# Causal mask as a GpSimd select after the exp, score steps in pairs, and one ring of six PSUM banks in a fused attention kernel

## The chip, the cores and the metric

One Trainium2 chip, one of its cores. The metric is the device time of one launch in microseconds, as the median of several runs; lower is better.

## The reference

The input x has 8 batches of 1024 tokens and 512 channels; it is normalised over the channels. On that, causal attention with 16 heads of 64 is computed, with two learned null keys and values for each head, and a layer norm of the normalised input is added (the second branch, of which only the norm term is computed here).

```python
q = (layernorm(x) @ Wq);  kv = x @ Wkv
k, v = concat(null_k, k), concat(null_v, v)
sim = 8 * l2norm(q) * q_scale @ (l2norm(k) * k_scale).T
sim = sim - slope[h] * abs(j - i)
sim = where(j > i, -inf, sim)
out = x + softmax(sim) @ v @ Wout + yn
```

## The kernel before

All of the work is in `fused_block`, written out by hand for each engine, with semaphores between them. Matmuls run on float16 in high and low parts: of each product three terms are taken (high by high, low by high, high by low).

A **unit** is one batch and one pair of heads, so there are 64 units (`NU`). A unit passes through these stages:

- Projection (`proj`, L1236 to L1238): 8 token tiles, each 12 matmuls of 388 columns into one PSUM bank. ScalarE (L566, L569) and VectorE (L1046, L1047) empty it.
- Norms of q and k: ScalarE squares (L584), VectorE sums (L1119, L1122), GpSimd takes the power and multiplies (L803, L809, L815, L820: the norm block), ScalarE and VectorE write the high and low float16 part (L574, L1054), a transposing DMA turns them into `KQ`.
- Pieces: a plain product of q and k (L1283), 12 pieces of 128 to 512 keys for each head, only to find each row's maximum. VectorE adds the distance term and takes the maximum (L1034), one operation per head and piece.
- Scores, ten steps m = 0 to 9 (`STEPS`), keys on the partitions and up to 512 queries in the free dimension: six matmuls with q and k (L1259) and two that add the distance term and minus the maximum (L1263), for each block of 128 keys. Heads 0 and 1 stand in rows 0 to 63 and 64 to 127 of TensorE and write to two neighbouring banks. Steps 2 and 9 hold two blocks each. Six steps (0, 1, 2, 7, 8, 9) hold the diagonal, eight blocks in all.
- The mask: for each of these blocks four matmuls of 64 columns (L1294) add -1e30 above the diagonal, with the tables `TRI` and `IDB`. They are issued after the pieces of the same slot.
- ScalarE takes the exp from PSUM into `PR`, float32 (L598), and directly behind it casts it to float16 into `PH` (L602). The low part `PL` is the difference: steps 0, 4 and 7 on GpSimd (L792), the others on VectorE (L1075). `PR` has two buffers, so the exp of step m+2 waits for the low part of step m.
- Values: three matmuls of 66, 64 and 66 columns for each block, head and query tile (L1322, L1324, L1326) into two banks `AV`. Null keys come first (L1305).
- Output projection, for each pair of units: 8 tiles of 6 matmuls of 512 columns (L1349 to L1351), added to `ACC` by VectorE (L1112).

The order of each engine's program is set by tables of slot numbers. A unit has 48 slots (`SL`); `due(s, W_...)` yields the items whose slot is s, so that stages of about four units are interleaved. Engines are not tied to each other by the slots, only by semaphores, and each runs its program strictly in order.

PSUM has eight banks. Two (`SB`) belong to the score steps: a step waits until the exp of the step before is done (`s_p`). Two belong to `AV`. Four are a ring for pieces, projections and output tiles: `ring_order` assigns the banks ahead of time, and `bank_free` waits for whoever reads the bank's last content.

## Time and profile before

| what | value |
|---|---|
| median of 3 runs | 2699.8 us (2696.74 to 2699.81) |
| profiled execution, span from first to last instruction | 2696.2 us |
| TensorE busy | 2622.8 us, 97% |
| VectorE busy | 2488.1 us, 92% |
| ScalarE busy | 2126.7 us, 79% |
| GpSimd busy | 2098.1 us, 78% |

The page gives the span of the profiled execution and no time of its own around it; the runs beside it lie 0.5 to 3.6 us above that span. Busy time is the union of an engine's instructions. Matmuls overlap, so a matmul's duration in a row is its way through the array, and how long it holds up the next one is seen from the starts.

### The profile page before, as it was taken

Reading aid. Unit: us, or ns where it says so; the run is one execution under the profiler, and the core shown is the slowest. Engines: PE = TensorE matmul, PEld = TensorE weight load, DVE = VectorE, ACT = ScalarE, POOL = GpSimd, SP = SyncE. Lnnn points to the kernel's source line nnn. Section 1 sums busy time; section 2 is a strip of 40 time slices with the busy share of each in tenths; the row PEclk is TensorE's granted clock in tenths of the full one; section 3 lists DMA queues with packets and bytes.
Section 4 is the critical chain, followed back from the end, with each engine's and each line's share of the span. In section 5 each row is a group of like instructions: output and inputs, shape, how many; then the busy total and the mean of one; then the engine's idle time right before and its main releaser. Section 6 shows DMA issues by size and latency. Waiting matters only on the chain.

```text
span 2696.2 us, 84329 instructions
## 1 busy us (share of the span) xinstructions
PE 2622.8 (97%) x31631; PEld 1575.9 (58%) x31631; DVE 2488.1 (92%) x6760; ACT 2126.7 (79%) x3385; POOL 2098.1 (78%) x2438
## 2 busy tenths in 40 slices
PE   5799999999999999999999999999999999999997
PEld 4455565565565565565555565565655665565654
...
GB/s 177 67 63 74 81 102 99 91 71 82 102 100 94 69 87 98 96 87 76 90 107 82 93 75 101 100 95 71 80 107 87 100 74 76 98 100 80 54 59 71
DMA packets 638790, 236.94 MB, mean 88 GB/s; under 512 B 594609, under 2 KB 596657, under 8 KB 638385
## 3 DMA queue, kind: packets, MB, share of 16 engines
q1 hardware_dynamic: 636912, 231.45, 39.6%
...
q10 hardware_dynamic: 1472, 0.09, 0.0%
...
## 4 chain that ended last, share of the span: by engine, by line
PE 81%; DVE 7%; issue 3%; DMA 2%; POOL 1%; SPq 1%; ACT 1%; DVEq 0%; POOLq 0%; ACTq 0%
PE PS L1259 12%; PE PS L1236 11%; PE PS L1238 10%; PE PS L1237 10%; PE PS L1283 6%; PE PS L1322 6%; PE PS L1326 4%; PE PS L1324 4%; PE PS L1263 4%; PE PS L1349 4%; PE PS L1350 3%; PE PS L1351 3%; DVE PS L1034 3%; DVE AR L1075 1%; PE PS L1294 1%
## 5 line engine op out<-in xcount | busy, mean ns | idle before, releaser
L1034 DVE CUSTOM_DVE_ANT_0 PS<-PS,STR 128x512 f32<-128x512 f32 (+3 forms) x1536 | 822.5, 580 | 121.9 <-PE PS L1283 114.9
L598 ACT ACTIVATE AR<-PS,SC 128x1024 f32<-128x1024 f32 (+1 forms) x640 | 655.1, 1024 | 143.5 <-PE PS L1294 75.7
L1236 PE MATMUL PS<-WH,XT 128*128 128x388 f16 x2048 | 676.7, 330 | 22.5 <-DVE AR L1047 13.5
L1237 PE MATMUL PS<-WL,XT 128*128 128x388 f16 x2048 | 673.9, 329 | 0.0
L1238 PE MATMUL PS<-WH,XT 128*128 128x388 f16 x2048 | 673.7, 329 | 0.0
L602 ACT ACTIVATE AR<-AR 128x1024 f16<-128x1024 f32 (+1 forms) x640 | 622.0, 972 | 20.3
L803 POOL TENSOR_TENSOR RN<-SS,HALF 128x8 f32<-128x8 f32 x256 | 453.6, 1772 | 182.7 <-DVE SS L1122 181.6
L1075 DVE TENSOR_TENSOR AR<-AR 128x768 f16<-128x768 f32 (+1 forms) x448 | 503.4, 1134 | 11.8 <-ACT AR L602 11.7
L1259 PE MATMUL PS<-AR 64*128 64x512 f16 (+3 forms) x4608 | 495.4, 324 | 9.1 <-ACT AR L598 8.9
L1322 PE MATMUL PS<-AR 128*128 128x66 f16 x4608 | 472.3, 195 | 1.8 <-DVE AR L1075 0.8
L1324 PE MATMUL PS<-AR 128*128 128x64 f16 x4608 | 468.8, 192 | 0.0
L1326 PE MATMUL PS<-AR 128*128 128x66 f16 x4608 | 466.3, 193 | 0.0
L1322 PEld LDWEIGHTS PS<-AR 128*128 128x128 f16 x4608 | 414.8, 97 | 71.5 <-issue 41.3
L792 POOL TENSOR_TENSOR AR<-AR 128x1024 f16<-128x1024 f32 x192 | 412.8, 2150 | 20.2 <-ACT AR L602 19.6
L1324 PEld LDWEIGHTS PS<-AR 128*128 128x128 f16 x4608 | 420.0, 99 | 8.6
L1326 PEld LDWEIGHTS PS<-AR 128*128 128x128 f16 x4608 | 420.3, 97 | 0.0
L566 ACT ACTIVATE QKB<-PS 128x128 f32<-128x128 f32 x512 | 139.7, 273 | 266.0 <-PE PS L1238 260.3
L1236 PEld LDWEIGHTS PS<-WH,XT 128*128 128x128 f16 x2048 | 200.5, 98 | 198.4 <-issue 55.6
L815 POOL TENSOR_TENSOR SQ<-QKB,RN 128x512 f32<-128x512 f32 x256 | 292.1, 1141 | 0.0
L796 POOL TENSOR_TENSOR OTK<-OTOK,OTK 128x512 f16<-128x512 f32 x128 | 163.1, 1275 | 152.5 <-ACT OTK L591 150.9
L1238 PEld LDWEIGHTS PS<-WH,XT 128*128 128x128 f16 x2048 | 201.0, 98 | 138.2 <-issue 2.9
L1259 PEld LDWEIGHTS PS<-AR 64*128 64x128 f16 x4608 | 199.6, 94 | 135.1 <-ACT AR L598 25.6
...
## 6 DMA issues: line engine op xcount, KB each, us to landing
XW<-in_L_attn_x SPq DMA_DIRECT2D x112, 256.0 KB, 3.0
...
AR<-QKB SPq DMA_TRANSPOSE x512, 2.5
...
```

The costliest lines, as they stand in the source:

```text
L598: e.activation(PR[:, n % 2, :, 0:wide], SB[:, :, 0:wide], ACT.Exp, scale=SIG).then_inc(s_p, 1)
L602: e.activation(PH[:, n % 3, :, 0:wide], PR[:, n % 2, :, 0:wide], ACT.Copy).then_inc(s_ph, 1)
L803: e.tensor_tensor(RN[:, i % 2, :], SS[:, i % 2, :], HALF[:, :], ALU.pow).then_inc(s_rn, 1)
L1034: e.tensor_tensor_reduce(out=r[:, 0:n], in0=r[:, 0:n], in1=ST[:, u % 2, h, o:o + n], scale=1.0, scalar=LOW, op0=ALU.add, op1=ALU.max, accu ...
L1075: e.tensor_tensor(PL[:, n % 3, :, 0:wide], PR[:, n % 2, :, 0:wide], PH[:, n % 3, :, 0:wide], ALU.subtract).then_inc(s_pl, 1)
L1236: e.matmul(to, XT[:, k, xs], WH[:, k, p, :], start=k == 0, stop=False)
L1237: e.matmul(to, XT[:, k, xs], WL[:, k, p, :], start=False, stop=False)
L1238: ins = e.matmul(to, XT[:, 4 + k, xs], WH[:, k, p, :], start=False, stop=k == KC - 1)
L1259: e.matmul(SB[:, h, to], KQ[hs, u % 2, a, ks], KQ[hs, u % 2, c, qs], start=(a, c) == (KH, QH) and not off, stop=False, skip_group_check=True)
L1322: e.matmul(AV[:, h, 66 * q:66 * q + 66], PH[:, n % 3, h, pq], VV[:, 0:66], start=False, stop=False, skip_group_check=True)
L1324: e.matmul(AV[:, h, 66 * q:66 * q + 64], PH[:, n % 3, h, pq], VV[:, 72:136], start=False, stop=False, skip_group_check=True)
L1326: ins = e.matmul(AV[:, h, 66 * q:66 * q + 66], PL[:, n % 3, h, pq], VV[:, 0:66], start=False, stop=kt == 4 * qc + q, skip_group_check=True)
```

## The change

- The mask matmuls and their tables go. After the exp, GpSimd sets the entries above the diagonal to zero in `PR` (`affine_select`, L817 of the changed kernel), one instruction for each of the six diagonal steps, over both heads and all blocks of the step. The cast of that step waits for it.
- The product that adds the distance term gets one more term for far entries (`FAR`, in `CTK` and `AL`); its matmuls stay the same in number and size.
- The exp and the cast of a step have separate slot tables (`W_SCORE`, `W_CAST`).
- `SB` goes. Pieces, projections, output tiles and score steps share a ring of six banks; `take_pair` gives a score step two neighbouring ones, and `bank_free` waits for their last readers.
- The 12 pieces are put in 10 groups; small ones share a pair of banks. The maxima of a group wait for its last matmul.
- All slot tables are new, and a unit has 50 slots.

```diff
-BANKS = 4
-SL = 48
+BANKS = 6
+SL = 50
...
-NEG = -1e30
 LOW = -3e38
+FAR = 32768.0
...
-PIECES = [(qt, c) for qt in range(NT) for c in range(1 + qt // 4)]
+GROUPS = [[(0, 0), (2, 0)], [(3, 0)], [(1, 0)], [(4, 0)], [(5, 0)], [(4, 1), (6, 1)], [(6, 0)], [(5, 1)], [(7, 0)], [(7, 1)]]
...
+DIAGONAL = [blocks[0][0] >= 4 * qc for qc, blocks in STEPS]
...
-W_PIECE = [47, 53, 56, 59, 66, 68, 69, 77, 79, 82, 83, 86]
-W_SCORE = [88, 96, 105, 108, 111, 115, 118, 126, 130, 133]
+W_PIECE = [54, 54, 61, 67, 68, 80, 80, 84, 92, 92]
+W_SCORE = [98, 98, 109, 109, 112, 112, 124, 124, 136, 136]
+W_CAST = [100, 101, 110, 111, 116, 116, 126, 127, 138, 142]
+W_CAUS = [101, 103, 109, 128, 136, 138]
...
-HOLD = [2.0, 2.1, 2.0, 6.7]
...
+HOLD = [11.9, 12.5, 14.5, 14.3, 14.8]
...
+def pieces(g):
+
+    out, at = [], 0
+    done = 2 * sum(len(z) for z in GROUPS[:g])
+    for qt, c in GROUPS[g]:
+        n = min(512, P * (qt + 1) - 512 * c)
+        out.append((qt, c, at, n, done))
+        at += n
+        done += 2
+    return out
 
...
+    def take_pair(slot, u, m):
+        i = min(range(BANKS - 1), key=lambda z: (max(read[z], read[z + 1]), read[z] + read[z + 1]))
+        for h in range(2):
+            who = ("sc", u, 2 * m + h)
+            at[who], before[who] = i + h, last[i + h]
+            last[i + h], read[i + h] = who, slot
+
...
-        SB, AV = PS[:, 0:2, :], PS[:, 2:4, 0:264]
+        AV = PS[:, 6:8, 0:264]
...
-                e.wait_ge(s_mx, 24 * u + i + 1)
+                e.wait_ge(s_mx, 24 * u + pieces(i // 2)[-1][4] + i % 2 + 1)
+            elif what == "sc":
+                e.wait_ge(s_p, NS * u + i // 2 + 1)
...
+                    low = BANK["sc", u, 2 * m]
                     w.wait_ge(s_st, 2 * n + 2)
                     w.wait_ge(s_wo, 8)
                     pl_done(w, n - 2)
-                    e.activation(PR[:, n % 2, :, 0:wide], SB[:, :, 0:wide], ACT.Exp, scale=SIG).then_inc(s_p, 1)
+                    e.activation(PR[:, n % 2, :, 0:wide], PS[:, low:low + 2, 0:wide], ACT.Exp, scale=SIG).then_inc(s_p, 1)
+                for u, m in due(s, W_CAST):
+                    n = NS * u + m
+                    wide = width(m)
                     w.wait_ge(s_p, n + 1)
+                    cut = causal(n)
+                    if DIAGONAL[m]:
+                        w.wait_ge(s_caus, cut + 1)
                     if n > 2:
                         w.wait_ge(s_av, n - 2)
...
+            for r in range(4):
+                pc(e.memset(CTK[0:64, :, r, 35 + 4 * r::64], FAR))
...
-            pc(e.memset(IDB[:, :], 0.0))
-            pc(e.affine_select(out=IDB[:, :], in_=IDB[:, :], compare_op=ALU.not_equal, fill=1.0, base=0,
-                               pattern=[[-1, P]], channel_multiplier=1))
-            pc(e.memset(TRI[:, :, :], 0.0))
-            for a in range(2):
-                pc(e.affine_select(out=TRI[:, a, :], in_=TRI[:, a, :], compare_op=ALU.is_ge, fill=NEG, base=64 * a - 64,
-                                   pattern=[[-1, P]], channel_multiplier=1))
-            pc(e.memset(TRI[0:64, :, :], 0.0))
-            pc(e.affine_select(out=TRI[0:64, 0, :], in_=TRI[0:64, 0, :], compare_op=ALU.is_ge, fill=NEG, base=0,
-                               pattern=[[-1, P]], channel_multiplier=1))
-            e.affine_select(out=TRI[0:64, 1, :], in_=TRI[0:64, 1, :], compare_op=ALU.is_ge, fill=NEG, base=64,
-                            pattern=[[-1, P]], channel_multiplier=1).then_inc(s_tri, 1)
             w.wait_ge(s_ready, 1)
...
+                for u, i in due(s, W_CAUS):
+                    m = [z for z in range(NS) if DIAGONAL[z]][i]
+                    n = NS * u + m
+                    two = len(STEPS[m][1])
+                    own = PR[:, n % 2, :, 0:256 * two].rearrange("p h (t c) -> p h t c", c=256)[:, :, :, 0:P]
+                    w.wait_ge(s_p, n + 1)
+                    e.affine_select(out=own, in_=own, compare_op=ALU.is_ge, fill=0.0, base=0,
+                                    pattern=[[0, 2], [0, two], [1, P]], channel_multiplier=-1).then_inc(s_caus, 1)
                 for u, m in due(s, W_PLOW):
...
+                        for h in range(2):
+                            far = ALF.rearrange("p (j k) -> p j k", k=P)[:, 4:8, 64:P]
+                            e.affine_select(out=far, in_=far, compare_op=ALU.not_equal, fill=-FAR, base=-(64 * h + 35),
+                                            pattern=[[-4, 4], [0, 64]], channel_multiplier=1).then_inc(s_ald, 1)
+                            w.wait_ge(s_ald, 2 + h)
...
-                    w.wait_ge(s_s, 24 * u + 2 * i + 2)
-                    w.wait_ge(s_str, 2 * u + 2)
-                    if u:
-                        w.wait_ge(s_m, 3 * (2 * (u - 1) + qt // 4) + 3)
-                    for h in range(2):
-                        r = rb("s", u, 2 * i + h)
-                        e.tensor_tensor_reduce(out=r[:, 0:n], in0=r[:, 0:n], in1=ST[:, u % 2, h, o:o + n], scale=1.0, scalar=LOW,
-                                               op0=ALU.add, op1=ALU.max,
-                                               accum_out=MX[:, qt // 4, qt % 4, h, c:c + 1]).then_inc(s_mx, 1)
+                    for qt, c, at, n, done in pieces(i):
+                        o = 896 - P * qt + 512 * c
+                        w.wait_ge(s_s, 24 * u + pieces(i)[-1][4] + 2)
+                        w.wait_ge(s_str, 2 * u + 2)
+                        if u:
+                            w.wait_ge(s_m, 3 * (2 * (u - 1) + qt // 4) + 3)
+                        for h in range(2):
+                            r = rb("s", u, 2 * i + h)
+                            e.tensor_tensor_reduce(out=r[:, at:at + n], in0=r[:, at:at + n], in1=ST[:, u % 2, h, o:o + n], scale=1.0,
+                                                   scalar=LOW, op0=ALU.add, op1=ALU.max,
...
+                for u, i in due(s, W_PIECE):
+                    bank_free(w, "s", u, 2 * i)
+                    bank_free(w, "s", u, 2 * i + 1)
+                    for qt, c, at, n, done in pieces(i):
+                        for g in range(qt // 2 + 1):
+                            w.wait_ge(s_kq[g], 32 * (u + 1))
+                        for h in range(2):
+                            hs = slice(64 * h, 64 * h + 64)
+                            e.matmul(rb("s", u, 2 * i + h)[:, at:at + n], KQ[hs, u % 2, QH, P * qt:P * qt + P],
+                                     KQ[hs, u % 2, KH, 512 * c:512 * c + n], start=not at, stop=True,
+                                     skip_group_check=True).then_inc(s_s, 1)
...
                     qc, blocks = STEPS[m]
-                    n = NS * u + m
-                    w.wait_ge(s_p, n)
+                    low = BANK["sc", u, 2 * m]
+                    bank_free(w, "sc", u, 2 * m)
+                    bank_free(w, "sc", u, 2 * m + 1)
                     for g in range(max(2 * qc + 1, blocks[-1][0] // 2) + 1):
...
-                                e.matmul(SB[:, h, to], KQ[hs, u % 2, a, ks], KQ[hs, u % 2, c, qs],
+                                e.matmul(PS[:, low + h, to], KQ[hs, u % 2, a, ks], KQ[hs, u % 2, c, qs],
                                          start=(a, c) == (KH, QH) and not off, stop=False, skip_group_check=True)
...
-                            ins = e.matmul(SB[:, h, to], AL[hs, kt - 4 * qc + 4, :], CT[hs, u % 2, qs], start=False,
-                                           stop=kt < 4 * qc, skip_group_check=True)
-                            if kt < 4 * qc:
+                            ins = e.matmul(PS[:, low + h, to], AL[hs, kt - 4 * qc + 4, :], CT[hs, u % 2, qs], start=False,
+                                           stop=True, skip_group_check=True)
+                            if kt == blocks[-1][0]:
                                 ins.then_inc(s_st, 1)
...
-                    if blocks[0][0] >= 4 * qc:
-                        w.wait_ge(s_tri, 1)
-                        for kt, off in blocks:
-                            for a in range(2):
-                                for h in range(2):
-                                    hs = slice(64 * h, 64 * h + 64)
-                                    to = slice(off + 64 * a, off + 64 * a + 64)
-                                    ins = e.matmul(SB[:, h, to], TRI[hs, a, :], IDB[hs, hs], start=False, stop=True,
-                                                   skip_group_check=True)
-                                    if a and kt == blocks[-1][0]:
-                                        ins.then_inc(s_st, 1)
...
-                    if blocks[0][0] == 0:
-                        w.wait_ge(s_nv2, 2 * u + qc + 1)
```

The orders below are of the middle of the program. First TensorE, around step 2 of a unit (two diagonal blocks). Before: L1236 to L1238 are projections, L1283 a piece, L1259 and L1263 scores, L1294 the mask, L1305 null keys.

```order
L1238 MATMUL PS<-WH,XT 128x388
L1283 MATMUL PS<-AR 128x384 x2
L1259 MATMUL PS<-AR 128x256 x6
L1263 MATMUL PS<-AR,AL 128x256 x2
L1259 MATMUL PS<-AR 128x128 x6
L1263 MATMUL PS<-AR,AL 128x128 x2
L1294 MATMUL PS<-IDB,TRI 128x64 x8
L1305 MATMUL PS<-VNT,PNT 128x264 x2
L1236 MATMUL PS<-WH,XT 128x388
```

Now, with L1274 as a projection, L1375 an output tile, L1316 and L1320 as scores, L1331 null keys, L1296 pieces, L1346 values:

```order
L1375 MATMUL PS<-WO,OT 128x512
L1316 MATMUL PS<-AR 128x256 x6
L1320 MATMUL PS<-AR,AL 128x256 x2
L1316 MATMUL PS<-AR 128x128 x6
L1320 MATMUL PS<-AR,AL 128x128 x2
L1316 MATMUL PS<-AR 128x512 x6
L1320 MATMUL PS<-AR,AL 128x512 x2
L1331 MATMUL PS<-VNT,PNT 128x264 x2
L1296 MATMUL PS<-AR 128x256 x2
L1346 MATMUL PS<-AR 128x66
```

The mask rows are gone, two steps follow each other with nothing between them, and the pieces stand by themselves.

ScalarE, with what each waits for. Before, L598 is the exp and L602 the cast (L566 and L569 empty a projection tile, L584 squares):

```order
L566 ACTIVATE QKB<-PS 128x128 [waits s_proj]
L569 ACTIVATE AR<-PS,VSC 128x2x64
L598 ACTIVATE AR<-PS,SC 128x2x384 [waits s_pl,s_st]
L602 ACTIVATE AR<-AR 128x2x384 [waits s_av,s_p]
L574 ACTIVATE QKB<-SQ 128x2x256 [waits s_t1]
L584 ACTIVATE SQ<-QKB 128x512 [waits s_hi,s_ss,s_lo,s_qb,s_kvev]
```

Now, L628 is the exp, L638 the cast, L595 and L598 empty a projection tile, L613 squares, L620 casts the output:

```order
L595 ACTIVATE QKB<-PS 128x128 [waits s_proj]
L598 ACTIVATE AR<-PS,VSC 128x2x64
L628 ACTIVATE AR<-PS,SC 128x2x384 [waits s_plp,s_st]
L628 ACTIVATE AR<-PS,SC 128x1024 [waits s_pl,s_st]
L638 ACTIVATE AR<-AR 128x2x384 [waits s_av,s_caus,s_p]
L638 ACTIVATE AR<-AR 128x1024 [waits s_av,s_p]
L613 ACTIVATE SQ<-QKB 128x512 [waits s_hi,s_ss,s_lo,s_qb,s_kvev]
```

Two exps come ahead of two casts, and the cast of a diagonal step waits for `s_caus`, the select.

GpSimd, with what each waits for: L817 is the select, L837 to L854 the norm block, L826 the low part of step 7.

```order
L817 AFFINE_SELECT AR<-AR 128x2x128 [waits s_p]
L837 TENSOR_TENSOR RN<-SS,HALF 128x8 [waits s_nsc,s_ss]
L843 TENSOR_TENSOR NSC<-QKB,RN 128x8 [waits s_rn]
L849 TENSOR_TENSOR SQ<-QKB,RN 128x512
L854 TENSOR_TENSOR SQ<-SQ,W2R 128x2x128 [waits s_t1]
L826 TENSOR_TENSOR AR<-AR 128x1024 [waits s_av,s_ph]
L817 AFFINE_SELECT AR<-AR 128x2x128 [waits s_p]
L817 AFFINE_SELECT AR<-AR 128x4x128 [waits s_p]
L837 TENSOR_TENSOR RN<-SS,HALF 128x8 [waits s_nsc,s_ss]
```

Before, the same engine has the norm block and the low part, and no select:

```order
L803 TENSOR_TENSOR RN<-SS,HALF 128x8 [waits s_nsc,s_ss]
L809 TENSOR_TENSOR NSC<-QKB,RN 128x8 [waits s_rn]
L815 TENSOR_TENSOR SQ<-QKB,RN 128x512
L820 TENSOR_TENSOR SQ<-SQ,W2R 128x2x128 [waits s_t1]
L731 TENSOR_TENSOR XHL<-XW,XHL 128x512 [waits s_xh]
L792 TENSOR_TENSOR AR<-AR 128x1024 [waits s_av,s_ph]
```

Three selects of a unit stand around a norm block and a low part that ran without them.

## Rows read from the trace of the kernel before

**Rows 1.** The page: busy time by engine, and the chain that ended last.

```profile
PE 2622.8 (97%) x31631; PEld 1575.9 (58%) x31631; DVE 2488.1 (92%) x6760; ACT 2126.7 (79%) x3385; POOL 2098.1 (78%) x2438
...
PE 81%; DVE 7%; issue 3%; DMA 2%; POOL 1%; SPq 1%; ACT 1%; DVEq 0%; POOLq 0%; ACTq 0%
```

**Rows 2.** Busy time in three stretches: PE, PEld, DVE, ACT, POOL, clock, DMA share, GB/s.

```profile
60.00:110.00 50.00, 29.20 (x141) 14.31 (x141) 45.56 (x109) 26.91 (x55) 25.98 (x31) 0.80 0.33 83
500.00:1000.00 500.00, 498.87 (x6111) 300.20 (x6109) 468.68 (x1287) 402.20 (x643) 401.86 (x465) 1.00 0.41 87
2640.00:2697.00 57.00, 42.75 (x647) 25.92 (x646) 33.78 (x71) 33.64 (x38) 25.47 (x22) 1.00 0.27 73
```

**Rows 3.** One line, the mask matmuls: duration min/median/max in ns, first and last start.

```profile
L1294 PE MATMUL PS<-IDB,TRI x2048: 187/190/190, 114.8 to 2680.1; 64*128 64x64 bf16 x187
```

**Rows 4.** Groups by line, TensorE: busy us, mean ns, then idle before and who ended it.

```profile
L1236 PE MATMUL PS<-WH,XT 128*128 128x388 f16 x2048 | 676.7, 330 | 22.5 <-DVE AR L1047 13.5 <-DVE MX L1018 6.7 <-DVE MX L1034 2.2
...
L1259 PE MATMUL PS<-AR 64*128 64x512 f16 (+3 forms) x4608 | 495.4, 324 | 9.1 <-ACT AR L598 8.9
...
L1283 PE MATMUL PS<-AR 64*128 64x512 f16 (+3 forms) x1536 | 258.2, 330 | 16.3 <-DVE MX L1034 12.5 <-DMA AR<-QKB 1.4 <-DVE ACC L1112 1.1
```

**Rows 5.** Timeline, TensorE, around 1009 us: start, duration, line.

```profile
1008.79 0.28 PE L1294 MATMUL PS<-IDB,TRI 64*128 64x64 bf16 x8
1008.90 0.28 PE L1305 MATMUL PS<-VNT,PNT 64*128 64x264 f16 x2
```

**Rows 6.** Timeline, TensorE, around 1011 us.

```profile
1010.77 0.33 PE L1237 MATMUL PS<-WL,XT 128*128 128x388 f16 x1
1010.93 0.33 PE L1238 MATMUL PS<-WH,XT 128*128 128x388 f16 x1
1011.19 0.39 PE L1283 MATMUL PS<-AR 64*128 64x512 f16 x2
1011.42 0.81 PE L1259 MATMUL PS<-AR 64*128 64x512 f16 x6
1012.06 0.38 PE L1263 MATMUL PS<-AR,AL 64*128 64x512 f16 x2
1012.38 0.20 PE L1322 MATMUL PS<-AR 128*128 128x66 f16 x1
```

**Rows 7.** Timeline, GpSimd: three selects of the program's start.

```profile
5.98 0.29 POOL L658 TENSOR_SCALAR_AFFINE_SELECT IDF<-IDF 128x128 f32<-128x128 f32 x1 [0.17 <-POOL IDF L657]
...
32.71 1.04 POOL L753 TENSOR_SCALAR_AFFINE_SELECT DS<-DS 128x1024 bf16<-128x1024 bf16 x1 [0.15 <-POOL DS L752]
...
52.21 0.67 POOL L771 TENSOR_SCALAR_AFFINE_SELECT IDB<-IDB 128x128 bf16<-128x128 bf16 x1
```

**Rows 8.** Groups by line, ScalarE and VectorE: exp, cast, low part.

```profile
L598 ACT ACTIVATE AR<-PS,SC 128x1024 f32<-128x1024 f32 (+1 forms) x640 | 655.1, 1024 | 143.5 <-PE PS L1294 75.7 <-PE PS L1263 57.7 <-POOL AR L792 5.2
L602 ACT ACTIVATE AR<-AR 128x1024 f16<-128x1024 f32 (+1 forms) x640 | 622.0, 972 | 20.3
...
L1075 DVE TENSOR_TENSOR AR<-AR 128x768 f16<-128x768 f32 (+1 forms) x448 | 503.4, 1134 | 11.8 <-ACT AR L602 11.7
```

**Rows 9.** Groups by line, GpSimd.

```profile
L803 POOL TENSOR_TENSOR RN<-SS,HALF 128x8 f32<-128x8 f32 x256 | 453.6, 1772 | 182.7 <-DVE SS L1122 181.6
L792 POOL TENSOR_TENSOR AR<-AR 128x1024 f16<-128x1024 f32 x192 | 412.8, 2150 | 20.2 <-ACT AR L602 19.6
L815 POOL TENSOR_TENSOR SQ<-QKB,RN 128x512 f32<-128x512 f32 x256 | 292.1, 1141 | 0.0
```

**Rows 10.** Groups by line, VectorE: two operations on SBUF.

```profile
L1054 DVE TENSOR_TENSOR QKB<-SQ,QKB 128x512 f16<-128x512 f32 x256 | 211.5, 826 | 2.9 <-ACT QKB L574 2.3
...
L1122 DVE SCALAR_TENSOR_TENSOR SS<-SS,CL 128x8 f32<-128x8 f32 x256 | 92.2, 360 | 8.8
```

**Rows 11.** Two lines of VectorE: duration min/median/max in ns.

```profile
L1122 DVE SCALAR_TENSOR_TENSOR SS<-SS,CL x256: 166/169/1285, 72.6 to 2632.0; 128x8 f32<-128x8 f32 x128
...
L1034 DVE CUSTOM_DVE_ANT_0 PS<-PS,STR x1536: 277/637/735, 85.2 to 2655.6; 128x512 f32<-128x512 f32 x128, 128x128 f32<-128x128 f32 x64
```

156 lines of the change are left out of this document (72 added, 84 removed).

## The prediction

> **What bounds the kernel now.** I read the page's busy shares first: TensorE 97%, VectorE 92%, ScalarE 79%, GpSimd 78% [rows 1]. A matmul's end is modelled and matmuls overlap, so 97% does not by itself say that TensorE is the limit. The table of stretches does: from 500 to 1000 us TensorE has 498.87 of 500 us, VectorE 468.68, ScalarE 402.20, GpSimd 401.86, all at the full granted clock (1.00, the 2.4 GHz level) [rows 2]. Only the two ends are different: in 60 to 110 us TensorE has 29.20 of 50, with the clock at 0.80 and VectorE at 45.56; in the last 57 us it has 42.75. So for some 2500 us TensorE's own work sets the pace, about 40 us for each of the 64 units (the mask matmuls of all units lie between 114.8 and 2680.1 us [rows 3]).
>
> The chain of waits agrees, 81% of it is TensorE [rows 1]. The groups by line tell how little it waits for others: 9.1 us before the score matmuls, nearly all for ScalarE's exp, 16.3 us before the pieces, nearly all for VectorE's max, 22.5 us before the projections, mostly for VectorE too [rows 4]. So the question for every edit is what it takes from or adds to TensorE's row, and whether it makes a wait that is not there now.
>
> **What the change takes from TensorE.** The mask matmuls, L1294: 2048 of 64 columns. Their row says 190 ns each [rows 3], but that is the time through the array, not the time they hold it up. That is read from starts: eight of them begin at 1008.79 and the next matmul begins at 1008.90 [rows 5], 0.11 us for eight, 14 ns each (rounding of the starts: 13 to 15). 2048 x 13.75 ns = 28 us. The eight stand between other matmuls on 64 rows, so no change of shape goes with them.
> A page would give more: the Trainium skill, TensorEngine Tiling (Array Packing), section Instruction Overhead, says that a matmul with one column takes as long as one with 60, about 60 cycles. At 2.4 GHz that is an estimate of 25 ns for each, 51 us for 2048, and the forecast would be 23 us lower. The row's 0.11 us for eight speaks against counting each alone, because the two heads' matmuls stand in different row halves and run together.
>
> The second cost is shape switches. Projection matmuls follow each other after 0.16 us (starts at 1010.77, 1010.93), yet L1283, on 64 rows, starts 0.26 us after the last of them, at 1011.19 [rows 6]. So a change from 128 rows to 64 costs 0.10 us. On the way back, a pair of 512 columns gives way to another on 64 rows after 0.23 us (1011.19, 1011.42), but to L1322 on 128 rows after 0.32 (1012.06, 1012.38): 0.09 again. Gathering score steps in pairs and pieces in groups ought to save such switches. Counted in the two orders, it hardly does: about 1284 before and 1276 now, 20 a unit in both, because pieces no longer ride along with a score step. 8 x 0.10 = 1 us.
>
> **Score steps in six banks.** Today a score step waits for the exp of the step before (one pair of banks). That has cost 9 us in all [rows 4]. The pair now comes from the ring, and two steps may stand in PSUM at once; ScalarE's order puts two exps ahead of two casts. But the same six banks also serve pieces, projections and output tiles, 4 of 6 can be held by two waiting score steps, and the bank may be one that VectorE has yet to read. Bounds: all 9.1 + 16.3 us of waits go, or as much comes back. I take 5 us off.
>
> **What GpSimd gets.** Six selects a unit, 384 in all: four over 2 x 128 elements and two over 4 x 128 per partition. The trace has no float32 select of that size. Nearest: 128 elements float32 0.29 us, 1024 bfloat16 1.04 us, so 0.84 ns an element and 0.40 and 0.61 us for ours; and 128 bfloat16 0.67 us, at a time when the tables of the program's start were being made [rows 7], 0.38 more, so 0.78 and 0.99 us. A unit gets 4 x 0.40 + 2 x 0.61 = 2.8 us, or at the high end 5.1 us; 64 units, 180 to 330 us. GpSimd's 2098 us become 2280 to 2430, 85 to 91% of the span. It is not the bound by its sum, so I count this at nothing. Its cover is ScalarE's slack of some 7 us a unit (402 of 500 us busy). A unit's steps are 4 us apart in the mean, and a diagonal step now takes exp, select, cast, low part: 1.0 + 0.5 + 1.0, and 1.1 on VectorE or 2.15 on GpSimd [rows 8, 9]; two float32 buffers allow 8 us between an exp and the end of its low part. What is late next if the cover goes is the cast, and behind it on ScalarE the evacuations that free the ring. The new waits on that queue are two: the cast for the select, and the pair of exps for the low part two steps back.
>
> **What VectorE gets.** The same 24 maxima, now read group by group; its sum does not move. But it shares something with GpSimd. L1122, 8 elements, has a median of 169 ns, yet a mean of 360 and a maximum of 1285; the max on PSUM (L1034) has 637 and at most 735 [rows 10, 11]. L1075, L1054 and L1122, 503 + 212 + 92 of 2696 us, 30%, are such operations on SBUF. If a select meets one in 30% of cases, VectorE loses 0.3 x 2.8 to 5.1 = 0.8 to 1.5 us a unit, on 37.5 (0.937 of 40). That stays below TensorE's 39.6, but a little will reach it through bank waits: 5 us in all.
>
> **Ends.** Building the two mask tables on GpSimd (L771 on, from 52.21 us) goes, and four short memsets and two selects on the position table come; VectorE is the busy one there [rows 2, 7], so 0. In the tail, exp, score and exp wait for each other in turn; pairs shorten that by a score step or two of about 1 us (1011.42 to 1012.38 [rows 6]), the selects lengthen it by 0.5 each: 0.
>
> **Sum** against the profiled span: 2696.2 - 28 - 1 - 5 + 5 = 2667.2 us. The page gives no time of its own around the span; the three runs have a median of 2699.8, 3.6 above it. So **2671 us**. A measurement of this kernel tells about 0.2% from no change, 5.4 us: 2694.4 to 2705.2 is "same".
>
> **Rivals.**
> 1. The rest of TensorE's waits goes as well, since a burst of score steps needs nothing and the ring has six banks: another 11 to 20 us beyond the forecast, down to 2650. For it: 25 us of waits named above. Against: the 16.3 us are VectorE's, which gets no faster.
> 2. The gain is eaten. TensorE's order is now lumpier (two score steps, then up to 48 value matmuls, then pieces that take four banks), and each group's maxima wait for its last matmul. A new wait of 0.2 to 0.45 us a unit gives back 13 to 28 us: 2682 to 2705.
> 3. VectorE becomes the bound by being shut out. If every select holds VectorE up for its whole length, VectorE has 37.5 + 2.8 = 40.3 us a unit against 40 now: 0.3 x 64 = 19 us slower, 2719. The max and the reads of PSUM, over half of its time, show no such effect, which speaks against "every".
> The Trainium skill, SBUF — State Buffer, section SBUF: two separate sides, states the rule: a VectorE operation with two SBUF inputs and a GpSimd operation that reads SBUF exclude each other for the whole instruction. By that rule, the trace agrees in L1122, whose 169 ns become up to 1285.
> 4. The select comes late: slower. GpSimd runs in order, and its norm block holds L803 and L815, 1.77 + 1.14 = 2.9 us, and two shorter ones [rows 9]; in the new order it stands right ahead of a unit's selects and of the low part of step 7, which the exp of step 9 waits for. If a select is late, the cast waits, and the evacuations behind it, and TensorE's next bank. It decides from 29/64 = 0.45 us a unit on TensorE. At one L815 a unit, 1.14 us, it costs 73 us: 2671 + 73 = 2744. Against it: GpSimd now waits 181.6 us for VectorE's sums before L803 [rows 9], so it is usually early.
> That the mask stays on TensorE is excluded: the new order has no such matmul.
>
> **How the numbers follow.** Forecast, 2660 to 2682: 0.42. Rival 1, below 2660: 0.13. Rival 2: 0.22, of which 0.12 still ends below 2694.4 and 0.10 within 0.2%. Rival 3: 0.08. Rival 4: 0.15. Faster 0.67, same 0.10, slower 0.23. The range 2652 to 2716 leaves out some 0.05 below and 0.15 above (most of rival 4 and the end of rival 3); by costs alone it is 2650 (all waits gone) to 2719.
>
> **What would show it.** Right: no bf16 matmul rows; TensorE's busy time down by 25 to 30 us; the stretch 500 to 1000 still at 497 or more; selects at 0.4 to 0.8 and 0.6 to 1.0 us, GpSimd at 85 to 91%; VectorE's busy time up by under 60 us, in L1122's and L1054's counterparts. Wrong: TensorE below 99% in the middle, with idle time before score or piece matmuls put down to exp or max; ScalarE's casts waiting for the select by more than 60 us in all; VectorE at 97% or more.

## Result, and the profile after

2925.0 us (median of 4 runs, 2918.8 to 2928.0) against 2699.6 before: ratio 1.0831, 95% interval 1.0814 to 1.0847. The change makes the kernel slower by 225 us; 2671 was forecast. The profiled execution has a span of 2922.6 us, 226.4 above the one before.

The page of the changed kernel, busy time by engine:

```profile
PE 2630.9 (90%) x29583; PEld 1510.3 (52%) x29583; DVE 2762.8 (95%) x6760; ACT 2089.0 (71%) x3385; POOL 2470.4 (85%) x2820
```

The stretches that answer to [rows 2] (same columns; the last is the program's end):

```profile
60.00:110.00 50.00, 20.62 (x97) 10.27 (x97) 33.94 (x71) 23.49 (x46) 20.26 (x22) 0.66 0.29 74
500.00:1000.00 500.00, 461.04 (x5245) 264.10 (x5240) 480.50 (x1186) 362.72 (x587) 432.02 (x487) 1.00 0.39 83
2850.00:2923.00 73.00, 54.84 (x690) 30.19 (x690) 46.16 (x83) 37.22 (x44) 38.72 (x38) 0.90 0.26 64
```

The mask's matmuls are gone (29583 in place of 31631), but TensorE's time isn't: in the middle it is busy for 461.04 of 500 us where it had 498.87, and the clock there is 1.00 in both. VectorE now has 480.50, up from 468.68, although it finishes fewer units in that time. So the bound has moved. By the starts of each unit's first projection matmul (L1236 before, L1274 after), unit 5 begins 22.8 us later than before, the 58 units from there to unit 63 take 2541.7 us in place of 2352.0 (43.8 each in place of 40.6), and from the start of unit 63 to the end it is 121.2 us in place of 107.4: 22.8 + 189.8 + 13.8 = 226.4.

The groups of the changed kernel by line, which answer to [rows 4, 8, 9, 10] (L1316 are the first score matmuls, L1296 the pieces, L628 exp, L638 cast, L1113 VectorE's low part, L826 GpSimd's, L817 the selects, L1092 and L1160 the counterparts of L1054 and L1122):

```profile
L628 ACT ACTIVATE AR<-PS,SC 128x1024 f32<-128x1024 f32 (+1 forms) x640 | 644.9, 1026 | 407.8 <-DVE AR L1113 198.5 <-PE PS L1320 116.8 <-POOL AR L826 89.8
L1113 DVE TENSOR_TENSOR AR<-AR 128x768 f16<-128x768 f32 (+1 forms) x448 | 638.1, 1435 | 9.4 <-ACT AR L638 9.4
L638 ACT ACTIVATE AR<-AR 128x1024 f16<-128x1024 f32 (+1 forms) x640 | 597.0, 967 | 35.2 <-POOL AR L817 18.3 <-PE PS L1350 11.1 <-issue 4.5
L1316 PE MATMUL PS<-AR 64*128 64x512 f16 (+3 forms) x4608 | 495.0, 325 | 37.3 <-DVE MX L1072 21.0 <-issue 12.6 <-DMA AR<-CTK 1.7
...
L837 POOL TENSOR_TENSOR RN<-SS,HALF 128x8 f32<-128x8 f32 x256 | 425.6, 1662 | 65.5 <-DVE SS L1160 61.4
L826 POOL TENSOR_TENSOR AR<-AR 128x1024 f16<-128x1024 f32 x192 | 424.8, 2213 | 16.7 <-ACT AR L638 14.6
...
L849 POOL TENSOR_TENSOR SQ<-QKB,RN 128x512 f32<-128x512 f32 x256 | 344.0, 1344 | 0.0
L1092 DVE TENSOR_TENSOR QKB<-SQ,QKB 128x512 f16<-128x512 f32 x256 | 279.5, 1092 | 14.6 <-ACT QKB L603 14.6
...
L817 POOL TENSOR_SCALAR_AFFINE_SELECT AR<-AR 128x256 f32<-128x256 f32 (+1 forms) x384 | 220.5, 574 | 233.2 <-ACT AR L628 229.2
...
L1296 PE MATMUL PS<-AR 64*128 64x512 f16 (+3 forms) x1536 | 210.6, 330 | 153.5 <-DVE ACC L1150 48.7 <-DVE AR L1085 42.6 <-ACT AR L628 35.6
...
L1160 DVE SCALAR_TENSOR_TENSOR SS<-SS,CL 128x8 f32<-128x8 f32 x256 | 105.7, 413 | 8.8
```

VectorE's low part takes 1435 ns in the mean where it took 1134, L1092 1092 where it took 826, and VectorE's busy sum rises from 2488.1 to 2762.8 us. Who waits is to be read in the idle columns: exp is idle for 407.8 us (143.5 before), 198.5 of them until VectorE's low part two steps back is done, 89.8 until GpSimd's; the pieces wait 153.5 us (16.3), and GpSimd's own idle time before L837 has shrunk from 182.7 to 65.5.

How an operation of VectorE becomes long shows in the timeline of VectorE, GpSimd and ScalarE at 905 us (start, duration, in brackets the wait ahead of it and who ended it):

```profile
905.55 2.13 POOL L826 TENSOR_TENSOR AR<-AR 128x1024 f16<-128x1024 f32 x1
...
905.71 3.05 DVE L1113 TENSOR_TENSOR AR<-AR 128x1024 f16<-128x1024 f32 x1
...
908.86 1.69 ACT L628 ACTIVATE AR<-PS,SC 128x768 f32<-128x768 f32 x2 [1.14 <-DVE AR L1113]
```

GpSimd starts its low part at 905.55 and has it until 907.68; VectorE starts the low part of the other step of the pair at 905.71 and ends 3.05 us later, at 908.76. The exp that needs its buffer has waited 1.14 us by then. By my count in the records of the trace, 59 of GpSimd's 192 low parts have a low part of VectorE beside them now, and 5 of 192 had one before. All 33 of VectorE's that are longer than 2.3 us are among these. The new order did that, and mostly for one pair: in 49 of the 59 GpSimd's step 7 stands beside VectorE's step 6, in 8 step 0 beside step 1, in 2 step 4 beside step 5.

These 59 do not carry the whole rise. By the same records a low part of VectorE with nothing of GpSimd's beside it takes 1.22 us (1024 elements) or 0.95 (768); what all 448 take above that sums to 164 us (29 before), and 63 of it lie in the 59. GpSimd's low parts also stand beside L1092 now, 62 times where it was 16, and L1092 takes 1918 ns in the mean there against 828 elsewhere. Others of GpSimd's operations lengthen VectorE's low part as well: beside L830 alone (the low part of the output) 1024 elements take 2.17 to 2.18 us, 12 times.

### The profile page after: what moved, and what is told of

Read it like the earlier page. It is cut to its first block and busy times, and to the rows that moved or that the text cites. A ratio compares the mean times of both kernels' runs of the same rounds, so it can differ in the third digit from the quotient of the medians.

```text
span 2922.6 us, 80374 instructions
## 1 busy us (share of the span) xinstructions
PE 2630.9 (90%) x29583; PEld 1510.3 (52%) x29583; DVE 2762.8 (95%) x6760; ACT 2089.0 (71%) x3385; POOL 2470.4 (85%) x2820
## 5 line engine op out<-in xcount | busy, mean ns | idle before, releaser
L628 ACT ACTIVATE AR<-PS,SC 128x1024 f32<-128x1024 f32 (+1 forms) x640 | 644.9, 1026 | 407.8 <-DVE AR L1113 198.5
L1072 DVE CUSTOM_DVE_ANT_0 PS<-PS,STR 128x512 f32<-128x512 f32 (+3 forms) x1536 | 812.1, 582 | 32.0 <-PE PS L1296 30.0
L1274 PE MATMUL PS<-WH,XT 128*128 128x388 f16 x2048 | 677.7, 331 | 12.0 <-DVE MX L1057 6.7
L1113 DVE TENSOR_TENSOR AR<-AR 128x768 f16<-128x768 f32 (+1 forms) x448 | 638.1, 1435 | 9.4 <-ACT AR L638 9.4
L638 ACT ACTIVATE AR<-AR 128x1024 f16<-128x1024 f32 (+1 forms) x640 | 597.0, 967 | 35.2 <-POOL AR L817 18.3
L1316 PE MATMUL PS<-AR 64*128 64x512 f16 (+3 forms) x4608 | 495.0, 325 | 37.3 <-DVE MX L1072 21.0
L1346 PE MATMUL PS<-AR 128*128 128x66 f16 x4608 | 469.8, 195 | 29.6 <-POOL AR L826 26.0
L1346 PEld LDWEIGHTS PS<-AR 128*128 128x128 f16 x4608 | 417.9, 97 | 132.7 <-issue 102.9
L837 POOL TENSOR_TENSOR RN<-SS,HALF 128x8 f32<-128x8 f32 x256 | 425.6, 1662 | 65.5 <-DVE SS L1160 61.4
L826 POOL TENSOR_TENSOR AR<-AR 128x1024 f16<-128x1024 f32 x192 | 424.8, 2213 | 16.7 <-ACT AR L638 14.6
L817 POOL TENSOR_SCALAR_AFFINE_SELECT AR<-AR 128x256 f32<-128x256 f32 (+1 forms) x384 | 220.5, 574 | 233.2 <-ACT AR L628 229.2
L1296 PE MATMUL PS<-AR 64*128 64x512 f16 (+3 forms) x1536 | 210.6, 330 | 153.5 <-DVE ACC L1150 48.7
L849 POOL TENSOR_TENSOR SQ<-QKB,RN 128x512 f32<-128x512 f32 x256 | 344.0, 1344 | 0.0
L1316 PEld LDWEIGHTS PS<-AR 64*128 64x128 f16 x4608 | 194.6, 94 | 232.7 <-issue 66.4
L1274 PEld LDWEIGHTS PS<-WH,XT 128*128 128x128 f16 x2048 | 200.3, 98 | 202.3 <-issue 51.1
L1092 DVE TENSOR_TENSOR QKB<-SQ,QKB 128x512 f16<-128x512 f32 x256 | 279.5, 1092 | 14.6 <-ACT QKB L603 14.6
```

The source lines that it names most:

```text
L628: e.activation(PR[:, n % 2, :, 0:wide], PS[:, low:low + 2, 0:wide], ACT.Exp, scale=SIG).then_inc(s_p, 1)
L638: e.activation(PH[:, n % 3, :, 0:wide], PR[:, n % 2, :, 0:wide], ACT.Copy).then_inc(s_ph, 1)
L837: e.tensor_tensor(RN[:, i % 2, :], SS[:, i % 2, :], HALF[:, :], ALU.pow).then_inc(s_rn, 1)
L1072: e.tensor_tensor_reduce(out=r[:, at:at + n], in0=r[:, at:at + n], in1=ST[:, u % 2, h, o:o + n], scale=1.0, scalar=LOW, op0=ALU.add, op1=A ...
L1113: e.tensor_tensor(PL[:, n % 3, :, 0:wide], PR[:, n % 2, :, 0:wide], PH[:, n % 3, :, 0:wide], ALU.subtract).then_inc(s_pl, 1)
L1274: e.matmul(to, XT[:, k, xs], WH[:, k, p, :], start=k == 0, stop=False)
```

## Experiments

Three theories stood at the start. A: GpSimd's operations on SBUF, the low parts above all, hold VectorE up, and VectorE bounds the new order. H (for handshake): the select between exp and cast costs, by its wait on a queue that works in order; the expectations of e1 to e3 call it theory B. The third, their theory C: the ring of six banks makes TensorE wait in order for banks that VectorE still reads. One more came up on the way: G, that GpSimd's time costs by itself.

### The parts of the change in the old order

**e1: the kernel before, with the selects in place of TensorE's mask.** Old order and banks, with a list for the cast and one for the select, whose places I chose and did not tune:

```diff
+W_CAST = [89, 97, 106, 109, 112, 116, 119, 130, 131, 134]
+W_CAUS = [90, 93, 95, 125, 125, 126]
...
+                    if DIAGONAL[m]:
+                        w.wait_ge(s_caus, cut + 1)
```

> The kernel before with one part of the change: mask matmuls out, six GpSimd selects a unit in, the cast in a slot of its own, everything else and all other slot tables as before. Theory A (VectorE is held up because the new order puts its operations on SBUF beside GpSimd's long ones; the selects are a small part): 2665 to 2710 us, VectorE's low part stays near 1134 ns in the mean. Theory B (the select between exp and cast costs the time): 2850 or more. Theory C (the ring of six makes TensorE wait): 2665 to 2710, since the ring is not in it.

Measured: 3026.8 us, ratio 1.1218 (1.1199 to 1.1238). GpSimd, by groups:

```profile
L802 POOL TENSOR_TENSOR AR<-AR 128x1024 f16<-128x1024 f32 x192 | 409.4, 2132 | 108.4 <-ACT AR L614 107.8
...
L793 POOL TENSOR_SCALAR_AFFINE_SELECT AR<-AR 128x256 f32<-128x256 f32 (+1 forms) x384 | 240.7, 628 | 262.7 <-ACT AR L604 240.5 <-PE PS L1328 20.2
```

It waits 240.5 us for exp ahead of the selects and 107.8 for casts ahead of its low parts, where it waited 19.6 before [rows 9]. The cover of 7 us a unit on ScalarE does not carry the handshake in this order. The places may have a part in it: on GpSimd the select of step 8 stands ahead of the low part of step 7 (both in slot 125), which the exp of step 9 waits for; in the changed kernel it stands behind it. Other places were not tried.

**e2: e1 with the ring of six banks as well.**

```diff
-BANKS = 4
-HOLD = [2.0, 2.1, 2.0, 6.7]
+BANKS = 6
+HOLD = [2.0, 2.1, 2.0, 6.7, 3.0]
...
-        SB, AV = PS[:, 0:2, :], PS[:, 2:4, 0:264]
+        AV = PS[:, 6:8, 0:264]
```

> As the first run, and with the one ring of six banks for score steps too, with the old slot tables, single steps and 12 pieces. Theory A: 2660 to 2720. Theory B: 2850 or more. Theory C: 2800 or more, with TensorE waiting before pieces and scores for the banks' last readers.

Measured: 3095.5 us, ratio 1.1472 (1.1449 to 1.1495), 69 us above e1. The ring costs here too.

**e5: the kernel before, with 8 selects a unit that nobody waits for**, over 256 elements of a tile of their own; they wait for nothing but each other. The mask stays on TensorE.

```diff
+                for u, i in due(s, W_CAUS):
+                    for z in ...:
+                        e.affine_select(out=SCR[:, :], in_=SCR[:, :], ...).then_inc(s_scr, 1)
```

> The kernel before, unchanged in its result, with eight additional selects a unit of 256 elements on a scratch tile on GpSimd, which wait for nothing and for which nobody waits. Handshake theory (the select costs because exp, select and cast wait for each other in three in-order queues): 2695 to 2720 us. GpSimd-time theory (the added 3 to 5 us a unit of GpSimd work, and what it takes from VectorE, is what costs): 2800 or more.

Measured: 2811.4 us, ratio 1.0416 (1.0399 to 1.0434), 112 us slower: the 2695 to 2720 that theory H gave is missed, and G's 2800 or more holds. Operations of GpSimd that nobody waits for cost 0.41 us here for each us of theirs (273.8 us).

**e6: e5 with each of these selects waiting for its step's exp**, still with nobody waiting for them.

```diff
+                    w.wait_ge(s_p, NS * u + (0, 1, 2, 7, 8, 9)[i] + 1)
```

> The same, with each of the additional selects waiting for the exp of its diagonal step; still nobody waits for them. If it is the waiting of GpSimd for the exp that costs (what is queued behind it there comes late): 2800 to 3000. If it is the cast's wait for the select: under 2740. First run of before with selects: 3027.

Measured: 2975.5 us, ratio 1.1023 (1.1007 to 1.1039), 164 us above e5. So of the handshake the half that the prediction did not price, GpSimd standing still with other work behind it, is by itself worth more than the selects' time, in the slots of e1. What it is worth in the changed kernel's slots was not measured by itself.

**e11: e5 with powers in place of the selects**, over 2 elements each. They were meant to keep GpSimd as busy and hardly to touch SBUF.

```diff
-                        e.affine_select(out=SCR[:, :], in_=SCR[:, :], ...)
+                        e.tensor_tensor(SCR[:, 0:2], TWOS[:, 0:2], HALF[:, 0:2], ALU.pow)
```

> As e5 (the kernel before with 8 more GpSimd operations a unit that nobody waits for, +112 us), but each is a power over 2 elements, about 0.45 us by a quarter of the 1.73 us for 8 elements in e8, in place of a select over 256 elements at 0.535 us. So it adds nearly the same GpSimd time and hardly touches SBUF. Theory G (GpSimd's time is what costs: its other work comes later and TensorE waits for it): +80 to +115 us, 2780 to 2815. Theory V (the selects cost by holding VectorE up): within 20 us of before, 2690 to 2720.

Measured: 2869.5 us, ratio 1.0632 (1.0616 to 1.0648), 170 us slower. The powers took longer than I had estimated:

```profile
L602 ACT ACTIVATE AR<-PS,SC 128x1024 f32<-128x1024 f32 (+1 forms) x640 | 655.6, 1024 | 242.0 <-POOL AR L802 80.2 <-PE PS L1304 74.8 <-PE PS L1273 55.6
...
L813 POOL TENSOR_TENSOR RN<-SS,HALF 128x8 f32<-128x8 f32 x256 | 460.9, 1800 | 46.3 <-DVE SS L1132 45.5
...
L802 POOL TENSOR_TENSOR AR<-AR 128x1024 f16<-128x1024 f32 x192 | 409.7, 2134 | 18.5 <-ACT AR L606 17.9
L794 POOL TENSOR_TENSOR SCR<-TWOS,HALF 128x2 f32<-128x2 f32 x512 | 408.3, 798 | 15.1
...
L1293 PE MATMUL PS<-AR 64*128 64x512 f16 (+3 forms) x1536 | 261.5, 333 | 93.5 <-DMA AR<-QKB 41.4 <-DVE MX L1044 33.6 <-issue 10.4
```

0.80 us each, 408.3 in all, and 170 / 408 = 0.42 us for each us, e5's rate again. So V (the expectation's name for the theory that the added operations cost by their own traffic on SBUF) falls, and it is GpSimd's time that costs. VectorE is not out of it: its sum rose by 108.4 us here and by 77.5 in e5. The largest part here, 51.9 us, is in L1064 (L1054 before, 826 ns, 1029 here). Of the 126 low parts of VectorE that stood beside a power, 98 took their own time, and the other 28 all had another operation of GpSimd beside them too; so the lengthening is put down to GpSimd's own operations, which came later and stood beside others of VectorE's. TensorE's busy sum rose as well, by 31.7 us in e5 and 56.8 here, at a mean granted clock of 0.984 and 0.979 in place of 0.993; that is a part of the 112 and the 170 us. The rows say how GpSimd's time gets through although it is busy for 78% of the span: its only large reserve, 182.7 us before the norm block [rows 9], is down to 46.3; exp waits 80.2 us for its low part (5.2 before [rows 8]), and the pieces 41.4 us for the transposes of QKB, whose scaling uses GpSimd's SQ (1.4 [rows 4]).

**e10: the kernel before without GpSimd's low parts** (from the second unit on a power over 8 elements stands in for each of steps 0, 4 and 7, so these low parts are missing from the values). The edit is that of e8, below.

> The kernel before, with the same replacement as e8 alone: GpSimd's low parts of steps 0, 4 and 7 left out from the second unit on, a power over 8 elements in their place. It tells whether e8's 155 us belong to the new order or to GpSimd's low parts anywhere. Theory A (pairs put GpSimd's low part beside VectorE's): the kernel before is bound by TensorE, which loses nothing: within 0.4% of before, 2688 to 2705, VectorE's low part (L1075, here shifted by a few lines) from 1134 to about 1090 ns. Rival (GpSimd's low parts hold the kernel up in any order): over 30 us faster.

Measured: 2699.8 us, ratio 1.0000 (0.9991 to 1.0010), VectorE's low part 1146 ns. As expected: where TensorE is the bound and hardly any low parts stand side by side (5 of 192), GpSimd's can go and nothing is gained.

**e7: the kernel before with the ring alone**, e2's edit without the selects.

> The kernel before with the one ring of six banks alone: mask on TensorE, single steps, 12 pieces, old slot tables. Ring theory: 2750 or more, with TensorE waiting before scores and pieces for VectorE's maxima. Otherwise 2690 to 2720.

Measured: 2819.4 us, ratio 1.0443 (1.0427 to 1.0459), 120 us slower, with VectorE no longer than before (88%). The score matmuls:

```profile
L1272 PE MATMUL PS<-AR 64*128 64x512 f16 (+3 forms) x4608 | 497.2, 324 | 100.1 <-DVE MX L1046 57.8 <-issue 35.3 <-ACT AR L610 2.0
```

They were idle for 9.1 us, nearly all for exp [rows 4]; now it is 100.1, the largest part for VectorE's maxima, which have yet to read the bank.

**e14: e7 with other estimates of how long a bank is held.**

```diff
-HOLD = [2.0, 2.1, 2.0, 6.7, 3.0]
+HOLD = [3.0, 3.1, 3.0, 6.7, 5.0]
```

> e7 (the kernel before with one ring of six banks and nothing else) with other estimates of how long a bank is held: 3.0 slots for pieces and outputs and 5.0 for scores, in place of 2.0 and 3.0. If e7's 120 us lie in which bank is given to whom, the time moves by over 25 us, either way. If they lie in the ring itself (TensorE, in order, waits for VectorE's maxima before scores that would have had a bank of their own), it stays within 25 us of 2819, and scores wait for VectorE's maxima as before, 60 to 130 us.

Measured: 3030.2 us, ratio 1.1225 (1.1205 to 1.1244), 211 us above e7; the same matmuls wait 256.4 us, 177.3 of them for maxima. So the cost lies in which bank is given to whom, and four numbers of a table moved it by 211 us. What a ring with good estimates costs or brings in the old order stays open.

### Taking parts out of the changed kernel

**e3: the changed kernel with the mask back on TensorE**, as before the change, and no selects.

```diff
-                for u, i in due(s, W_CAUS):
-                    e.affine_select(out=own, in_=own, ...).then_inc(s_caus, 1)
...
+                                    ins = e.matmul(PS[:, low + h, to], TRI[hs, a, :], IDB[hs, hs], start=False, stop=True,
```

> The changed kernel with the mask put back on TensorE (2048 matmuls of 64 columns right behind the scores) and without the selects and the cast's wait for them; pairs, ring and slot tables as changed. Theory A: 2850 to 2950, VectorE's low part still over 1300 ns in the mean. Theory B: under 2760. Theory C: 2850 to 2950.

Measured: 2849.2 us, ratio 1.0559 (1.0538 to 1.0581), at the lower edge of A's range and far from H's: 76 us better than the change, 150 worse than before. The exchange of the mask, which is the change's first aim, loses 76 us in the new order, and two thirds of the loss are there without it. VectorE is still at 2698.6 us (95%) with a low part of 1418 ns.

**e8: the changed kernel without GpSimd's low parts** of steps 0, 4 and 7 from the second unit on; a power over 8 elements stands in their place, and they are missing from the values.

```diff
-                        e.tensor_tensor(PL[:, n % 3, :, 0:wide], PR[:, n % 2, :, 0:wide], PH[:, n % 3, :, 0:wide],
-                                        ALU.subtract).then_inc(s_plp, 1)
+                        e.tensor_tensor(DUM[:, 0:8], TWOS[:, 0:8], HALF[:, :], ALU.pow).then_inc(s_plp, 1)
```

> The changed kernel with GpSimd's low part (three a unit, 2.2 us each) replaced from the second unit on by a power over 8 elements, about 1.7 us, that hardly touches SBUF; those low parts are left out. Theory A (VectorE held up by GpSimd's long SBUF operations beside it): VectorE's low part falls from 1435 ns to 1250 or less, the counterpart of L1054 from 1092 to 900 or less, the time to 2740 to 2840. Otherwise 2880 or more.

Measured: 2769.9 us, ratio 1.0261 (1.0240 to 1.0281), 155 us better than the change. But 1.7 us stood for 2.2, so GpSimd's time had changed as well. (e4 was the same with the power in the first unit too; it has no measured time.)

**e13: e8 with a power over 11 elements**, so that GpSimd's time stays.

```diff
-                        e.tensor_tensor(DUM[:, 0:8], TWOS[:, 0:8], HALF[:, :], ALU.pow).then_inc(s_plp, 1)
+                        e.tensor_tensor(DUM[:, :], TWOS[:, :], TWOS[:, :], ALU.pow).then_inc(s_plp, 1)
```

> The changed kernel with its selects, and from the second unit on a power over 11 elements in place of each of GpSimd's low parts (those low parts are left out of the values). In e8 the power over 8 elements took 1.73 us and moved the time by 155 us, but it was also 0.5 us shorter than the low part; by the slope from 2 elements (0.80 us, e11) to 8 (1.71 us) 11 take about 2.17 us, the low part's own 2.21. So GpSimd's time stays and only its traffic on SBUF goes. Theory A (VectorE held up): nearly all of e8's gain stays, 2765 to 2810, VectorE's low part (L1113, shifted) under 1250 ns. Theory G (GpSimd's time, at about 0.41 us for each us as in e5 and e11): the gain is gone, 2880 to 2925, though VectorE's low part is short.

Measured: 2776.8 us, ratio 1.0286 (1.0271 to 1.0301). The groups:

```profile
L630 ACT ACTIVATE AR<-PS,SC 128x1024 f32<-128x1024 f32 (+1 forms) x640 | 637.8, 1026 | 259.7 <-PE PS L1327 131.6 <-POOL DUM L831 85.6 <-DVE AR L1120 38.1
...
L1120 DVE TENSOR_TENSOR AR<-AR 128x768 f16<-128x768 f32 (+1 forms) x448 | 525.2, 1181 | 12.5 <-ACT AR L640 12.5
...
L831 POOL TENSOR_TENSOR DUM<-TWOS 128x11 f32<-128x11 f32 x189 | 414.9, 2195 | 12.3 <-ACT AR L640 10.5
...
L1303 PE MATMUL PS<-AR 64*128 64x512 f16 (+3 forms) x1536 | 200.6, 329 | 60.5 <-DVE ACC L1157 17.8 <-DMA AR<-QKB 16.9 <-ACT AR L630 16.5
...
L1099 DVE TENSOR_TENSOR QKB<-SQ,QKB 128x512 f16<-128x512 f32 x256 | 183.5, 717 | 14.9 <-ACT QKB L605 14.9
```

2195 ns stand for 2213, GpSimd is as loaded (86%), and 148 of e8's 155 us stay. Two rows of the timeline, at 864 us, set against the pair at 905 us above:

```profile
863.91 2.11 POOL L831 TENSOR_TENSOR DUM<-TWOS 128x11 f32<-128x11 f32 x1
...
865.01 1.22 DVE L1120 TENSOR_TENSOR AR<-AR 128x1024 f16<-128x1024 f32 x1
```

The same low part over 1024 elements beside an equally long operation of GpSimd takes 1.22 us, not 3.05. By my count 112 of the 120 low parts beside such a power keep their own time, and the other 8 have another operation of GpSimd beside them too. VectorE's sum falls by 252.4 us to 2510.4. This is the run that decides between A and G in the new order: A. It exchanges the operation along with its size (a power over 11 elements for a subtraction over 1024), so that it is the traffic on SBUF, and not the kind of operation, is the likely reading and not shown apart.

**e12: the changed kernel with GpSimd making steps 0, 1 and 7.**

```diff
-PL_POOL = (0, 4, 7)
+PL_POOL = (0, 1, 7)
```

> The changed kernel with one number changed: GpSimd makes the low parts of steps 0, 1 and 7 in place of 0, 4 and 7, so that only one of its three stands beside the low part that VectorE makes of the other step of its pair. The result stays the kernel's. Theory A in its narrow form (the collision is with the partner's low part): VectorE's low part falls from 1435 ns to about 1320, 40 to 90 us faster, 2835 to 2885. In its wide form (GpSimd's 2.2 us hold up whatever VectorE does beside them): the hold moves to other operations, and the time stays within 40 us of 2925. Rival (the wait is what counts: GpSimd makes two low parts one after the other, and the values and the next exp wait for the second): slower, 2940 to 3000, exp waiting for GpSimd's low part over 150 us.

Measured: 2885.0 us, ratio 1.0687 (1.0669 to 1.0705), 40 us better than the change. VectorE's low part falls to 1394 ns only, and VectorE's sum by 63 us. Between the narrow form of A (40 to 90) and the wide one (within 40), it sits on the border. It does not test the pairing, though: by the same count as above 55 of GpSimd's low parts still have one of VectorE's beside them (59 in the changed kernel), all of them step 7's beside step 6's, which the edit left alone. What it took away is the company of L1092: 8 meetings with GpSimd's low part in place of 62, and 238.2 us in all in place of 279.5.

**e15: the changed kernel with all low parts on VectorE**, `PL_POOL = ()`.

> The changed kernel with one list emptied: VectorE makes all ten low parts, GpSimd none. The result stays the kernel's. GpSimd loses 425 us of work, VectorE gets 192 low parts at about 1.2 us, 230 us, and loses the hold of about 150 to 230 us. Theory A: VectorE's busy time stays near 2750 us and so does the bound, 2850 to 2940, with VectorE's low part under 1250 ns. Theory G: clearly faster than 2850, since GpSimd's time is what costs. Rival (VectorE comes later with the values' inputs): over 2940, values waiting for VectorE's low part over 60 us.

Measured: 3002.4 us, ratio 1.1124 (1.1104 to 1.1144), 77 us worse than the change: outside the ranges of both A and G.

```profile
L1113 DVE TENSOR_TENSOR AR<-AR 128x1024 f16<-128x1024 f32 (+1 forms) x640 | 835.0, 1314 | 7.6 <-ACT AR L638 7.5
...
L628 ACT ACTIVATE AR<-PS,SC 128x1024 f32<-128x1024 f32 (+1 forms) x640 | 650.8, 1028 | 535.7 <-DVE AR L1113 371.7 <-PE PS L1320 160.1 <-issue 0.3
...
L1296 PE MATMUL PS<-AR 64*128 64x512 f16 (+3 forms) x1536 | 213.2, 332 | 227.2 <-ACT AR L628 121.8 <-DVE ACC L1150 45.2 <-DVE AR L1085 42.2
```

VectorE's sum came out as A had it (2777.0 us), but its low part takes 1314 ns, not under 1250, and exp waits 371.7 us for it: the chain from exp to cast to low part and back to exp through the two float32 buffers now runs through the busiest engine at each step. It was the wait, the kind of rival named, though on exp and not on the values (31.6 us).

**e9: the changed kernel with neither selects nor GpSimd's low parts** (e3's and e8's edits together; these low parts are missing from the values).

> The changed kernel with both of its suspected costs taken away: the mask is back on TensorE (as in e3), and from the second unit on GpSimd's low parts of steps 0, 4 and 7 are left out, a power over 8 elements, which touches hardly any memory, standing in their place (as in e8; so those low parts are missing from the values). Theory A (VectorE is held up by GpSimd's long operations on SBUF, and the selects' cost is apart from it): the gains add, 2925 - 76 (e3) - 155 (e8) = 2694, range 2670 to 2715; VectorE's low part (L1118) mean under 1200 ns, TensorE 96% or more. Rival B (both experiments free the same thing, GpSimd's time or VectorE's): they overlap, and the time stays at 2740 to 2770. Rival C (the ring and the order cost by themselves, whatever GpSimd does, as e7 had +120): not under 2760, TensorE under 95% with VectorE not lengthened.

Measured: 2751.1 us, ratio 1.0185 (1.0167 to 1.0203). The gains overlap, as rival B had it: 174 us in place of 76 + 155 = 231. Both free VectorE or what waits for it. The middle is nearly whole again:

```profile
60.00:110.00 50.00, 20.41 (x95) 10.30 (x95) 33.84 (x70) 23.37 (x45) 19.97 (x21) 0.66 0.29 74
500.00:1000.00 500.00, 490.79 (x5999) 289.84 (x5996) 471.30 (x1274) 386.41 (x632) 401.25 (x456) 1.00 0.41 85
```

VectorE's low part takes 1318 ns even so, where under 1200 was expected, because GpSimd's other operations stand beside it. What is left, 55.4 us of span against before, stands in the starts of the units: unit 5 begins 18.6 us late, the middle takes 33.1 more (41.1 us a unit in place of 40.6), the end 3.6 more. The 18.6 belong to what e9 keeps of the new order, tables, pairs and ring together: in 60 to 110 us VectorE has 33.84 us of work where it had 45.56 [rows 2], and the granted clock is at 0.66 (0.80 before). The ring alone in the old order (e7) makes unit 5 4.9 us late.

## Why the prediction was wrong

Its sum was -28 - 1 - 5 + 5 around a bound that stays TensorE. The sign of the whole hangs on two terms that were counted at next to nothing, and the experiments name both.

- **"What VectorE gets": the step that failed.** It was to be 0.8 to 1.5 us a unit, 37.5 rising to at most 39, "below TensorE's 39.6". Measured: VectorE's sum rose by 274.7 us, 4.3 us a unit. The price of a meeting was right in kind (L1122's 169 ns becoming up to 1285 [rows 11] is the same effect), but only the new selects were counted as what VectorE meets. They are not what does it: with them gone (e3) VectorE is still up by 210 us. What changed is the company of operations that were there before: GpSimd's low part, 2.2 us, beside VectorE's 59 times in place of 5, and beside L1092 62 times in place of 16. The prediction had both orders before it and counted in them shape switches, not which long operations of the two engines come to stand side by side. e13 puts 148 of the 225 us on these low parts, at an unchanged time of GpSimd.
- **"What GpSimd gets": counted at nothing, wrongly.** The selects' own time was sized well enough: 0.48 us over 256 elements and 0.76 over 512 (220.5 us in all, 180 to 330 forecast), GpSimd at 85% of a longer span. Its sum rose by 372.3 us to 2470.4, above the 2280 to 2430 forecast, because its other operations lengthened too (L849 by 52 us). The cover was not there. In the old order each us of GpSimd's time costs 0.41 to 0.42 us (e5, e11), and waiting for exp cost 164 us more in the slots of e6. In the changed kernel taking the selects out brings 76 us with the mask matmuls back on TensorE (e3), and 19 us where GpSimd's low parts are out already (e8 to e9). What those matmuls cost in it, where TensorE is not the bound, no run shows.
- **"Score steps in six banks": -5, bounds 25.4 either way.** The bounds were too narrow. By itself in the old order the ring costs 120 us, and 329 with other estimates (e7, e14). The mechanism, a bank that VectorE has yet to read, was named in the step; its size was taken from waits of an order in which it hardly arose. What the ring costs within the changed kernel stays open: its order of score steps rests on six banks, and a version with the old ones was not tried.
- **"Ends": 0.** They cost 22.8 us up to unit 5 and 13.8 after the start of unit 63. Of these 18.6 and 3.6 are still there without selects and GpSimd's low parts (e9).
- **The mask matmuls: -28.** Not contradicted, and not shown in the time either, since TensorE no longer sets it. The 2048 rows are gone; TensorE's busy sum is nevertheless 8.1 us above before. Overlapping matmuls are counted once in it, so fewer overlaps would do that; no run was made for it. In e13, which has the mask on GpSimd too and fewer waits, the sum is 2604.6, 18.2 below before. The 14 ns for each matmul stay an estimate from one place of the trace.
- **The rivals.** None held the result. Rival 3, VectorE as the bound, was right about the engine and gave 2719: it priced one meeting for each select. Rival 4, cast and exp late behind GpSimd, ran beside it: casts wait 18.3 us for the select, below its sign of 60, while exp waits 89.8 for GpSimd's low part. Of the signs for "wrong", the first came true (TensorE at 92% in the middle), the other two did not: VectorE stopped at 96% there, short of 97, as the waits around it keep it from filling.
- **The rule.** The Trainium skill, SBUF — State Buffer, section SBUF: two separate sides, says that a VectorE operation with two SBUF inputs and a GpSimd operation that reads SBUF exclude each other for the whole of the first one's length. By that rule, the timeline at 905 us agrees: 905.55 + 2.13 us of GpSimd, and VectorE ends 1.08 us after it, near the 1.22 us that it takes alone. The pair at 864 us in e13 does not: the power reads SBUF as well and lasts 2.11 us, and VectorE's operation is no longer than alone, so there the measurement decides. The prediction cited the rule and applied it to six new operations, not to the ones that moved.
